# Other queue orders around the routing of block 7, where the experts' tiles begin

## What is computed

```
h = layernorm(x) * (1 + ca) + sa
x = x + ga * attn(h)                  # a gated scan, then a SiLU feed-forward of 768
h = layernorm(x) * (1 + cb) + sb
s = softmax(h @ router)               # 8 experts
out = sum over the two best experts e of s[e] * ((gelu(h @ w1[e]) * (h @ v1[e])) @ w2[e])
x = x + gb * (out + bias)
```

## Time and profile before

| | |
|---|---|
| time, median of 3 runs | 848.93 us (848.23 to 850.63) |
| time of the profiled execution | 848.34 us |
| its span, first to last instruction | 846.2 us |
| PE busy | 818.6 us (97%) |
| DVE busy | 557.7 us (66%) |
| POOL busy | 485.8 us (57%) |
| ACT busy | 367.9 us (43%) |
| granted PE clock, mean | 0.996 |

### The profile page before, as it was taken

One profiled execution on the slowest core, in us unless ns is written; L12 is line 12 of the kernel. 1 busy time (PEld: TensorE's weight loads), 2 busy tenths in 40 slices (PEclk: granted clock), 3 DMA queues, 4 the chain that ended last, 5 costly groups with the idle time before them and its releaser, 6 DMA issues.

```text
span 846.2 us, 18804 instructions
## 1 busy us (share of the span) xinstructions
PE 818.6 (97%) x5006; PEld 724.6 (86%) x5007; DVE 557.7 (66%) x1534; ACT 367.9 (43%) x681; POOL 485.8 (57%) x454
## 2 busy tenths in 40 slices
PE   8899999999999999978999999999999999999995
PEld 4679898988889879757999999999999999999994
DVE  6788777878876848775555655555655565565553
ACT  5884657565564525534224234224233242342221
POOL 2353645868685877569645646537537465383332
PEclk9999999999999999999999999999999999999998
DMA  8141050303021172327532432523324322222221
GB/s 281 34 113 50 2 181 9 119 26 102 14 90 45 58 233 62 142 78 199 153 47 40 137 45 37 150 44 113 68 38 137 51 37 44 38 38 38 38 45 25
DMA packets 49983, 67.64 MB, mean 80 GB/s; under 512 B 4944, under 2 KB 44240, under 8 KB 49936
## 3 DMA queue, kind: packets, MB, share of 16 engines
q1 hardware_dynamic: 36272, 47.71, 18.4%
q0 software_dynamic: 13664, 19.35, 12.2%
HBM read 43.51 MB, written 23.54 MB: 79 GB/s over the span
## 4 chain that ended last, share of the span: by engine, by line
PE 87%; POOL 3%; DVE 3%; issue 1%; ACT 1%; DMA 1%; another core or an unknown queue 0%; ACTq 0%; DVEq 0%; POOLq 0%
PE ps L614 24%; PE ps L616 24%; PE ps L615 24%; PE ps L776 5%; PE ps L742 2%; PE ps L715 1%; POOL routed L2009 1%; DMA out_rows<-y_moe,tok_moe 1%; PE ps L819 1%; PE ps L818 1%; PE ps L660 1%; PE ps L702 1%; PE ps L632 1%; PE ps L667 1%; POOL out_rows L2031 1%
## 5 line engine op out<-in xcount | busy, mean ns | idle before, releaser
L614 PE MATMUL ps<-split,xT_moe_hi 128*128 (+2 forms) x426 | 165.5, 388 | 0.1
L616 PE MATMUL ps<-split,xT_moe_hi 128*128 (+2 forms) x426 | 160.1, 376 | 0.0
L615 PE MATMUL ps<-split,xT_moe_lo 128*128 (+2 forms) x426 | 159.8, 375 | 0.0
L2021 POOL TENSOR_TENSOR y_moe<-y_moe 128x256 f32<-128x256 f32 x69 | 65.9, 956 | 122.8 <-DVE y_moe L1653 122.6
L1174 ACT ACTIVATE hidT_hi<-ps 128x768 fp32r<-128x768 f32 x70 | 56.9, 813 | 177.7 <-PE ps L776 168.6
L2031 POOL DMA_INDIRECT out_rows<-y_moe,tok_moe x71 | 111.1, 1564 | 28.9 <-issue 22.5
L1168 ACT ACTIVATE gelu_moe<-ps 128x704 f32<-128x704 f32 x71 | 53.8, 758 | 133.6 <-PE ps L616 126.9
L614 PE MATMUL ps<-split,hidT_hi 128*128 (+1 forms) x355 | 99.9, 281 | 1.3 <-DVE y_moe L1653 0.7
L615 PE MATMUL ps<-split,hidT_lo 128*128 (+1 forms) x355 | 100.1, 282 | 0.0
L616 PE MATMUL ps<-split,hidT_hi 128*128 (+1 forms) x355 | 99.9, 281 | 0.0
L1970 POOL TENSOR_TENSOR hid_lo<-hf_sb,hid_hi 128x512 fp32r<-128x512 f32 x48 | 67.1, 1399 | 50.8 <-ACT hid_hi L1146 50.7
(11 more groups left out here) (232 smaller groups left out, 1993.9 us busy)
## 6 DMA issues: line engine op xcount, KB each, us to landing
raw<-in_w SPq DMA_DIRECT2D x9, 1408.0 KB
x_moe<-routed SPq DMA_DIRECT2D x74, 132.5 KB
raw<-in_w SPq DMA_DIRECT2D x9, 640.0 KB
x_again<-in_x SPq DMA_DIRECT2D x8, 512.0 KB
out_rows<-x_again SPq DMA_DIRECT2D x8, 512.0 KB
x_sb<-in_x SPq DMA_DIRECT2D x7, 512.0 KB, 3.9
gu_raw<-in_gu_t SPq DMA_DIRECT2D x1, 1536.0 KB, 8.9
raw<-in_w SPq DMA_DIRECT2D x18, 64.0 KB
```

The costliest lines, as they stand in the source:

```text
L614: pe.matmul(dst, a_hi, b_hi, start=first, stop=False)
L615: pe.matmul(dst, a_lo, b_hi, start=False, stop=False)
L616: return pe.matmul(dst, a_hi, b_lo, start=False, stop=last)
L2021: g.tensor_tensor(y_moe[:, t.slot, 0, :], y_moe[:, t.slot, 0, :], y_moe[:, t.slot, 1, :], ALU.add)\
```

## The change

It reorders the calls in the lists of PE, ACT and DVE and changes where PE fills. POOL's and SP's lists stay. On DVE slots(6) and weigh(6) move ahead of multiply(Tile(1)), count(7) moves behind weigh(7) and hidT_rest(2), table() behind multiply(3) and xT_rest(4), the three splits of expert 0 to places from multiply(4) on, and tile 4's hidT_rest ahead of xT_rest(Tile(5)). On ACT router_exp(6) moves ahead of gelu(Tile(1)) and gelu(Tile(2)) ahead of h2_copy(7, 1). On PE 27 fills become 13, rank_tokens(6) and (7) and x_transposes(3) and (4) move forward, and hid_transposes(4) and second_product(4), which tile_step(5) had done, stand in the list ahead of x_transposes(5).

```diff
             def tile_step(t):
                 e = entry(pe, TAB_EXPERT, t, E - 1)
-                hid_transposes(t.near(-1))
-                if t.n > EARLY and not final(t):
-                    x_transposes(t.near(1))
+                if t.n > EARLY:
+                    hid_transposes(t.near(-1))
+                    if not final(t):
+                        x_transposes(t.near(1))
                 first_products(t, e)
                 if t.n == EARLY:
                     x_transposes(t.near(1))
-                second_product(t.near(-1), PICKED if t.n == EARLY else pe.snap(kept, min_val=0, max_val=E - 1))
+                else:
+                    second_product(t.near(-1), pe.snap(kept, min_val=0, max_val=E - 1))
                 pe.reg_mov(kept, e)
...
             first_products(Tile(1), PICKED, AB[2:])
-            pe.wait_ge(gelu_r, 2)
-            fill(0, 3)
+            rank_tokens(6)
             x_transposes(Tile(2))
             second_product(Tile(0), PICKED)
-            rank_tokens(6)
+            pe.wait_ge(gelu_r, 2)
+            fill(0, 8)
             hid_transposes(Tile(1))
             first_products(Tile(2), PICKED, AB[:2])
-            pe.wait_ge(hid_r, 2)
-            fill(2, 4)
             h2_transposes(7, 0)
             first_products(Tile(2), PICKED, AB[2:])
             h2_transposes(7, 1)
+            x_transposes(Tile(3))
             router_logits(7)
-            x_transposes(Tile(3))
             second_product(Tile(1), PICKED)
-            fill(RING, 5)
+            rank_tokens(7)
             hid_transposes(Tile(2))
-            rank_tokens(7)
             first_products(Tile(3), PICKED, AB[:2])
+            first_products(Tile(3), PICKED, AB[2:])
             count_all()
-            first_products(Tile(3), PICKED, AB[2:])
-            fill(RING, 4)
+            x_transposes(Tile(4))
             second_product(Tile(2), PICKED)
-            x_transposes(Tile(4))
-            fill(RING, 4)
-            table_transposes()
-            pe.wait_ge(gelu_r, 4)
-            fill(0, 7)
             hid_transposes(Tile(3))
             first_products(Tile(4), PICKED, AB[:2])
+            table_transposes()
             first_products(Tile(4), PICKED, AB[2:])
             second_product(Tile(3), PICKED)
+            hid_transposes(Tile(4))
+            second_product(Tile(4), PICKED)
+            pe.wait_ge(gelu_r, 5)
+            fill(0, 5)
             x_transposes(Tile(5))
...
             hidT_split(Tile(0))
+            router_exp(6)
             gelu(Tile(1))
             xT_split(Tile(2))
-            router_exp(6)
-            hidT_split(Tile(1))
             split_hi(act, 0, 0)
             split_hi(act, 0, 1)
+            hidT_split(Tile(1))
             h2_copy(7, 0)
+            gelu(Tile(2))
             h2_copy(7, 1)
-            gelu(Tile(2))
             xT_split(Tile(3))
+            split_hi(act, 0, 2)
             router_exp(7)
-            split_hi(act, 0, 2)
             hidT_split(Tile(2))
...
             gelu(Tile(4))
+            hidT_split(Tile(4))
             xT_split(Tile(5))
-            hidT_split(Tile(4))
...
             norm2_stats(7)
+            slots(6)
+            weigh(6)
             multiply(Tile(1))
             xT_rest(Tile(2))
             norm2_centre(7)
             norm2_scale(7)
-            slots(6)
-            weigh(6)
+            hidT_rest(Tile(1))
             gate_y(Tile(0))
             count(6)
-            hidT_rest(Tile(1))
             multiply(Tile(2))
             choose(7)
-            count(7)
             xT_rest(Tile(3))
-            take_gates(Tile(2), expert)
             slots(7)
             weigh(7)
             hidT_rest(Tile(2))
+            count(7)
             gate_y(Tile(1))
+            take_gates(Tile(2), expert)
+            multiply(Tile(3))
+            xT_rest(Tile(4))
             table()
-            split_lo(v, 0, 2)
-            xT_rest(Tile(4))
-            multiply(Tile(3))
-            split_lo(v, 0, 0)
-            table_out()
             hidT_rest(Tile(3))
             gate_y(Tile(2))
-            split_lo(v, 0, 1)
+            table_out()
             multiply(Tile(4))
-            xT_rest(Tile(5))
+            split_lo(v, 0, 0)
             take_gates(Tile(3), expert)
             gate_y(Tile(3))
+            hidT_rest(Tile(4))
+            split_lo(v, 0, 1)
+            xT_rest(Tile(5))
             take_gates(Tile(4), expert)
-            hidT_rest(Tile(4))
+            split_lo(v, 0, 2)
             take_gates(Tile(5))
```

## The result

The changed kernel took 856.47 us (median of 5 runs, 854.95 to 858.74) against 848.93 for the kernel before: a ratio of 1.0085, 95% interval 1.0059 to 1.011. It is slower by 7.5 us. The forecast was 844.8, with 0.10 for slower. The prediction was wrong. The later runs show more than that: the sign of this change depends on a condition that no edit set, and under the other condition the same kernel is 0.26% faster by the medians.

A forecast was written before the change was run, and what follows sets the result against it. TensorE, full from 403 us on, was bound by waits and fills before that, 14.4 us of room. Of two chains joining at hid_transposes(6), POOL's decides: 4.1 us off 848.34 gives 844.2, on the median 844.8; range 841.8 to 848.7.

The forecast's parts named there:

- I take the signal at no delay: Between rank_tokens(7) and slots(7): PE's signal, 3.4 us late before, was counted as on time; 3.4 us kept as other end.
- Rival (b): PE's signals late again between rank_tokens(7) and slots(7): gain only 0.7 us, time 848.2, chance 0.20.
- the clock at full: Sign to look for: a wait of about 2.3 us ahead of second_product(4) without the clock dropping.
- 2.3 + 0.9 + 0.9 us of wait: New PE waits: 2.3 us ahead of second_product(4), 0.9 each at tile 5's rows and at hid_transposes(5).
- the fills saved: On PE, 27 fills become 13: 14 fewer at 0.22 us each, 3.1 us less work.
- POOL's term: Through block 7's scatters and tile 2's add to multiply(6): 4.1 us sooner; 0.7 with the late signal in full.
- 2.0 forecast: slots(7) sooner by order: of 5.4 us in all, 2.0 are the order and 3.4 the late signal.
- The row decided rightly: Profile row: a scatter beside DVE's split takes 2.51 us, neighbours 0.96, so moving splits away saves 1.8 us of stretch.
- the join: At hid_transposes(6) PE's chain (395.8) and POOL's (multiply(6) at 397.9) meet; the later counts, 4.1 us sooner.
- Tile 5's rows cost nothing: On PE: tile 5's rows arrive near 379, and PE is not there before 382.
- 5.3 forecast: Sum of PE's new waits in the stretch from 346.6 to 403.0 us, against 8.5 before.
- Rival (d): Clock halves in the wait ahead of second_product(4): about 9 us more, 853.8, chance 0.07.

The follow-up runs named there:

- session 3: Runs on one chip, no late signals: kernel before 844.23 us (25 runs), the unedited changed kernel 0.9974 times that.
- session 4: Runs on one chip, 12 to 16 late signals: kernel before 848.68 us (18 runs), the unedited changed kernel 1.0074 times that.
- session 1: Runs on one chip, 14 to 17 late signals: kernel before 848.09 us (35 runs); changed kernel with tile 4's move undone 1.0006.
- back_split: Changed kernel with tile 4's products back behind tile 5's rows and one split put beside block 7's scatters; 0.9984 times the kernel before, no late signals.
- back_again: Changed kernel with only tile 4's products back behind tile 5's rows, run without late signals; 0.9967 times the kernel before.
- after_again: The changed kernel unedited, run without late signals; 0.9974 times the kernel before.
- before_third: The kernel before, unedited, run without late signals; ratio 1.0004 to the kernel before.
- before_again: The kernel before, unedited, run with late signals; ratio 1.0006 to the kernel before.

## Why the prediction was wrong

**The step that failed.** "I take the signal at no delay, for it is later than its instruction in this one stretch". The stretch was not the only one: the same trace has 17 late signals up to 385 us, around the scatters of every block from the first on. The delay goes with the burst, so advancing the signal past block 6's burst did save slots(7) its lag (367.16, right behind the rank products), as forecast. But the logits, now in the tail of that burst, paid 2.3 us, and choose(7) came at 364.89 instead of 359.7; of the other 2.9 us, 1.4 had passed before hid_transposes(0). Then, beside block 7's burst, which keeps its close pace because the splits were moved away from it, second_product(2), hid_transposes(3) and both halves of first_products(4) are 4.2, 6.4, 5.2 and 3.9 us late. Rival (b) named the mechanism but looked for it at one place and priced it as a gain not had; that it could lose had a share of the 0.10 and no price. The second step that failed is the clock: the sum has no term for it, and the sign to look for was "the clock at full".

How much: from session 3 to session 4 the start of hid_transposes(6) in the changed kernel moves from 395.28 to 407.67. 2.0 us of that lie ahead of the stretch (hid_transposes(0) starts at 338.6 and 340.6), so it loses 10.4 us where signals are late, waits and clock together. The kernel before pays, from session 3 to session 1, 401.53 - 396.66 less 1.6 = 3.3 us. The difference of 7.1 us is 0.84% of the time, against 1.0% between the ratios 0.9974 and 1.0074.

**Tile 4's move.** The prediction put 2.3 + 0.9 + 0.9 us of wait on it and took the fills saved and POOL's term as cover. Its waits were well sized: 2.16, 1.27 and 0.95 us. What failed is the cover. In the session of the result PE's chain, not POOL's, set the end, so every wait counted; five fills now stood bare too, at the lower clock. Undoing the move gained 0.8% between the result's session and session 1, and nothing in session 3.

**The other terms, by session 3.** 13 fills and no scatter over 1.1 us, as forecast. The times are counted from hid_transposes(0), so 1.1 us come off each difference. choose(7) is 0.7 us later, not 0.2 sooner; slots(7) is 1.1 us sooner by order (2.0 forecast). The last scatter ends at 371.8 instead of 375.8, 2.9 us sooner (7.1 - 3.4 = 3.7 without the late signal). The add of tile 2 comes at 385.19 against 386.21, which is 0.1 us later (4.1 - 3.4 = 0.7 sooner). So in these two traces, with no signal late, POOL's term is nothing.

Of block 7's scatters those beside a split are stretched: in back_split the split stands at 372.55 to 374.31 and the scatter issued at 373.11 takes 2.03 us, ending 0.83 us after it; in the earlier trace rows the split ends at 376.66 and the scatter beside it at 377.49, 0.83 us after it again. The row decided rightly against the inference of the Trainium skill (SBUF — State Buffer) that a `tensor_tensor` on VectorE doesn't hold up descriptor generation; the rows don't tell whether the scatter waits with its descriptors or with reading its row numbers (slot_i). The same page states that a `tensor_tensor` with both inputs in SBUF contends with GpSimd's reads; by that, the trace agrees: in the changed kernel the split beside result_base(7) and a sum takes 3.61 us, against 1.60 for a split of that size in session 3, and the sum 2.77 against 1.3. The next split, beside another sum of 2.77 us, takes 1.75.

**Wrong at the join.** The prediction had POOL's add of tile 2 decide the end, with PE held at hid_transposes(6). The kernel before has that wait where signals are late; no traced run of the changed kernel has it. In the kernel before without late signals the chain of 365 to 400 us goes through the scatters and the gather of tile 5's rows:

```profile
by line: POOL routed L2009 23.4%; PE ps L614 14.8%; PE ps L615 14.4%; PE ps L616 14.4%; issue 9.7%; DMA routed<-rows,slot_i 7.4%; PE ps L776 6.2%; DMA x_moe<-routed 6.0%; PE ps L742 3.1%; SPq L499 1.4%; PE ps L818 0.7%; PE ps L819 0.7%; SPq
```

PE's wait for those rows is 1.6 us there and 3.95 in back_again. "Tile 5's rows cost nothing" still holds in the changed kernel, where tile 4's products and five fills stand ahead of them: neither the result nor after_again has a wait for them. In after_again PE decides: its waits after 354 us sum to 0.47 + 0.64 + 2.32 + 1.27 + 0.95 = 5.65 us against the 5.3 forecast, those of the kernel before to 4.6, and 14 fills less are 3.1 us, which would make it 2.0 us sooner. The lower clock takes most of it: PE is busy at it for 6.7 us from hid_transposes(0) to (6), against 3.4 in before_third, and half of the difference is 1.6 us.

**The clock.** Rival (d), with a chance of 0.07 and outside the range, came true in part: 6.6 us (estimated above) against the 9 it was given. The clock was low from 341.6 us, ahead of every moved call; from 382.6, in the wait of 5.33 us ahead of second_product(3); and from 392.8, behind the wait of 2.16 ahead of second_product(4). By the same estimate the 10.4 us between sessions 3 and 4 are 7.6 of idle time (5.8 to 13.4), 2.6 of clock (3.3 to 5.9) and 0.2 of other work. In the kernel before, from before_third to before_again, the idle time grows by 4.2 us (4.6 to 8.7) and the clock's share falls from 1.7 to 0. So more than half of the 7.1 us by which late signals cost the changed kernel more is clock, 4.3 us, in single traces. The medians over the runs point the same way: the mean clock of the changed kernel is 0.995 in session 3 and 0.9885 in session 4, that of the kernel before 0.994 and 0.9935. That the late signals' waits are what lowered it is likely, not shown.

## What to carry to other kernels

Where a trace shows an engine starting well after the product it waits for, look for every such gap before counting on its absence: the gaps here follow bursts of indirect DMAs, so a reorder moves them onto other work rather than removing them. Consumers of results made beside such a burst want slack, that is other work between product and use; the fills and the second product standing in the way were that slack, which is a reading of the lists and not an experiment. Look at the granted clock over the whole stretch before calling fills a cost: without its 27 the kernel before was no faster, because the work ran slower. Measure a change of 0.5% in more than one session, each against its own runs of the kernel before: the sign of this one turned.

## What the runs showed of the hardware

Signals of PE come up to 6.4 us late near a burst of indirect DMAs 1.27 us apart, in the traces of some sessions and in none of others; one signal of DVE is late by up to 1.1 us in four of them, and none of ACT. With 2.3 us from one to the next none is late by over 0.5 us beside that burst. The same chip showed both behaviours at different times. The cause is not known.
